# Weight check in three pieces, one logarithm scale per lane, rstd for four sequences at once, down copy on GpSimd, the branch turned round and a new order

## The chip, the cores and the metric

The kernel runs on one core of a Trainium2 chip. The metric is the device time of one execution in microseconds (us). A core has four compute engines with a queue each: TensorE (PE; its weight loads are PEld), VectorE (DVE), ScalarE (ACT) and GpSimd (POOL). SyncE (SP) issues most of the DMAs. Each queue runs in the order in which it is written, and waits on semaphores.

## The reference

```python
x = x + _wkv(time_decay, time_first, _layernorm(x), ctx_2048)      # (16, 128, 256)
x = x + _ffn(_layernorm(x), gate_w, up_w, down_w, gate_s, up_s, down_s)

# _wkv, for each sequence and channel, over the 128 steps:
w = -exp(time_decay); u = time_first; aa = bb = 0; pp = -1e38
q = maximum(pp, u + k_t)
y_t = (exp(pp - q) * aa + exp(u + k_t - q) * v_t) / (exp(pp - q) * bb + exp(u + k_t - q))
q2 = maximum(pp + w, k_t)
aa = exp(pp + w - q2) * aa + exp(k_t - q2) * v_t
bb = exp(pp + w - q2) * bb + exp(k_t - q2);  pp = q2

# _ffn: 256 -> 704 -> 256
hdn = silu((x @ gate_w.T) * gate_s) * ((x @ up_w.T) * up_s)
out = (hdn @ down_w.T) * down_s
```

The three weight matrices are drawn from -1, 0 and 1.

## The kernel before

The 16 sequences are cut into eight units of two sequences (256 tokens), and into four groups of two units (512 tokens) for the feed-forward part. A call such as `expk(3)` is one step of unit 3, `gate(7)` one step of tile 7. The hidden size 704 makes six tiles a group (five of 128, one of 64 for gate and up together), so tiles are numbered 0 to 23, six to a group.

For each unit: DVE takes the statistics of the layer norm (`stats1`, `aggr1`, lines 459 to 469); ACT makes the reciprocal standard deviation by a logarithm and an exponential (`rstd1`, L327, L329); POOL makes the bias (`bias1`, L234, L236); ACT takes exp of the normalised input (`expk`, L336) and POOL multiplies it by the values in units 0 to 3 (`weigh`, L242). PE transposes both (`e_T`, L600, and `p_T`, L609). DVE runs the recurrence as two scans (`scan_e`, L487, and `scan_p`, L498) and makes denominator and numerator (`denom`, L512, and `numer`, L522). ACT makes the reciprocal of the denominator as exp of minus the logarithm (`log_den`, L347, and `recip`, L354; one instruction for each half of the channels, since scale and bias differ between the halves). POOL multiplies and adds (`divide`, L258, and `add_y`, L264), which ends the first residual. Then PE transposes it (`x1_T`, L619), DVE takes the second statistics (`stats2`, `aggr2`), POOL or ACT the reciprocal standard deviation (`rstd2`, `rstd2a`), ACT normalises (`norm2`, L370), PE transposes back (`n_T`, L627), and ACT and DVE split the result into a high and a low part for the matmuls (`high_n`, L381, and `low_n`, L545).

The feed-forward part of a tile is `gate` and `up` (four matmuls of 512 columns each, L645), `silu` (ACT, L406), `gated` (DVE, L559), `high_h` (ACT, L417), `low_h` (POOL, L294), and `down` (four matmuls, L660); `finish` (DVE, L574) adds the second residual and SP stores it. `gate(0)` needs `low_n(0)` and `low_n(1)` and the rounded copy of the gate and up weights; `down(0)` needs that of the down weights.

The matmuls may use a faster number format only when the low 16 bits of every weight are zero, which is tested at run time. `wcheck` (ACT, L392) sums the low halves of the gate and up weights, then of the down weights; `wany_` (DVE, L453), `count` (PE, L668 and L669) and `publish` (DVE, L457) make one number of it. PE reads it into a register and branches (L695, L696). Its program from there on stands twice: the first body is for weights that are not exact, the second for exact ones. These weights are exact, so the second body runs:

```python
found = pe.value_load(flag[0:1, 0:1], min_val=0, max_val=2 * P)
with pe.If(found > 0):
    rest_of_program(False)
with pe.Else():
    rest_of_program(True)
pe.nop()
```

Before the branch PE does `e_T` and `p_T` of units 0 and 1 and `count`. The copies of the weights in the faster format are made by `whi`: the gate and up weights in four pieces on POOL (L286), the down weights in one on ACT (L397). The order of all steps on each engine is written out by hand (lines 297 to 303, 421 to 432, 577 to 588 and 681 to 689). ACT loads its function tables (L308) whenever it passes between exp or logarithm and silu.

Of the kernel before, what the change touches and what calls it, by code (L numbers as in the profile page):

```python
# [17 lines left out]
UB = 2  # L18
# [17 lines left out]
F_MAX = 55.0  # L36

# [13 lines left out]
def build(nc, x_tok, x_ch, v_tok, v_ch, w_gu, w_d, vecs, out_ch):  # L51
    with ExitStack() as ctx:
# [170 lines left out]
        def _(pool):  # L223
# [73 lines left out]
            bias1(0); weigh(0); bias1(1); weigh(1); whi(0); whi(1); whi(2); whi(3); first(0); divide(0); bias1(2)  # L297
            add_y(0); bias1(3); divide(1); add_y(1); weigh(2); bias1(4); weigh(3); rstd2(0); first(1); first(2)
            rstd2(1); divide(2); add_y(2); rstd2(2); divide(3); add_y(3); low_h(0); bias1(5); low_h(1); bias1(6)
            rstd2(3); low_h(2); divide(4); add_y(4); low_h(3); rstd2(4); divide(5); low_h(4); add_y(5); low_h(6)  # L300
            bias1(7); rstd2(5); low_h(7); first(3); divide(6); add_y(6); low_h(8); low_h(9); rstd2(6); low_h(10)
            divide(7); add_y(7); low_h(12); low_h(13); low_h(14); rstd2(7); low_h(15); low_h(16); low_h(18); low_h(19)
            low_h(20); low_h(21); low_h(22)

        @block.scalar
        def _(act):
# [24 lines left out]
            def expk(u):

                act.wait_ge(s_xt[u], 16)
                act.wait_ge(s_nb1, u + 1)
# [4 lines left out]
            def log_den(u):  # L339
                act.wait_ge(s_den, u + 1)  # L340
                if u == 0:
                    act.wait_ge(s_f, 2)
                if u >= 2:
                    act.wait_ge(s_y, u - 1)
                for c in range(CC):
                    q = slice(c * UB, (c + 1) * UB)
                    last = nc.scalar.activation(rden[:, u % 2, q, 1:T], den[:, u % 2, q, 1:T], ACT.Ln, scale=elift[:, c:c + 1])  # L347
                last.then_inc(s_ln, 1)

            def recip(u):  # L350
                act.wait_ge(s_ln, u + 1)
                for c in range(CC):
                    d = rden[:, u % 2, c * UB:(c + 1) * UB, 1:T]
                    last = nc.scalar.activation(d, d, ACT.Exp, scale=-1.0, bias=lift[:, c:c + 1])  # L354
                last.then_inc(s_rd, 1)
# [28 lines left out]
            def wcheck(k):  # L384

                act.wait_ge((s_wgu, s_wd)[k], 16)
                raw = wgu[:, :, :, :].rearrange("p c m n -> p (c m n)") if k == 0 else wd[:, :, :].rearrange("p m n -> p (m n)")
                n = (WGU_N, WD_N)[k]
# [354 lines left out]
```

## Time and profile before

| | us |
|---|---|
| median of 3 runs | 114.91 |
| lowest, highest | 114.43, 115.06 |
| the profiled execution, its own time | 114.74 |
| its span in the trace | 112.9 |
| PE, DVE, ACT, POOL busy | 83.7, 80.9, 83.7, 66.5 |
| TensorE's mean granted clock, of full speed | 0.977 |

The span runs from the first to the last record of the trace; the 1.8 us that are left lie around it. Busy times are of one execution; the time of a matmul is modelled, and matmuls overlap, so that the distance between two starts tells more than the duration of one. A letter q behind an engine (PEldq, SPq) marks its sequencer. "Issue" in a chain is time in which an engine waited for nothing that the profile shows.

### The profile page before, as it was taken

How to read it: one execution, taken by the hardware profiler on the slowest of the kernel's cores; microseconds unless marked ns; L12 is line 12 of the kernel's file. 1: busy time of each engine (PE TensorE's matmuls, PEld its weight loads, DVE VectorE, ACT ScalarE, POOL GpSimd, SP SyncE). 2: the span in 40 equal slices, each digit the busy share in tenths (PEclk: the TensorE clock that was granted, in tenths of full speed). 3: DMA queues.
4: the chain of work that ended last, by engine and by line, in shares of the span. 5: the costliest groups of instructions: out<-in, count | busy, mean ns of one | idle time of the engine just before them, and what ended most of it. 6: DMA issues, size and time to landing. Idle time of an engine off the chain costs nothing.

```text
span 112.9 us, 1463 instructions
## 1 busy us (share of the span) xinstructions
PE 83.7 (74%) x380; PEld 64.9 (57%) x380; DVE 80.9 (72%) x169; ACT 83.7 (74%) x157; POOL 66.5 (59%) x100
## 2 busy tenths in 40 slices
PE   0034700039249999997999989999999999999940
PEld 0022400039139778766688858876877777888810
DVE  1918989409997999997899999999385266515270
ACT  4453999941998989899999989999984763555500
POOL 2025956890683259889559485795898720473600
PEclk9999999999976999999999999999999999999996
DMA  2999999991000000000000005000040000500005
GB/s 71 275 378 397 386 355 377 370 367 62 4 3 0 0 0 9 0 0 0 0 0 0 0 0 186 6 3 0 0 175 14 0 0 0 192 0 0 0 0 186
DMA packets 6458, 10.77 MB, mean 95 GB/s; under 512 B 560, under 2 KB 3632, under 8 KB 6320
## 3 DMA queue, kind: packets, MB, share of 16 engines
q1 hardware_dynamic: 6304, 10.62, 26.3%
q8 instruction: 5, 0.08, 0.3%
q10 hardware_dynamic: 144, 0.03, 0.2%
q14 instruction: 5, 0.04, 0.1%
HBM read 8.55 MB, written 2.10 MB: 94 GB/s over the span
## 4 chain that ended last, share of the span: by engine, by line
PE 35%; ACT 23%; POOL 13%; issue 10%; DMA 8%; DVE 6%; SPq 1%; DVEq 1%; POOLq 0%; ACTq 0%
PE ps_f L645 20%; PE ps_d L660 9%; DMA wgu<-w_gu 8%; POOL hl L294 3%; POOL yk L258 3%; ACT L308 3%; ACT rden L354 3%; ACT ek L336 3%; ACT junk L392 3%; ACT rden L347 2%; POOL xc L264 2%; PE ps_x L627 2%; ACT sil L406 2%; DVE sbe L487 2%; PE ps_a L600 2%
## 5 line engine op out<-in xcount | busy, mean ns | idle before, releaser
L645 PE MATMUL ps_f<-xh,wgu_r 128*128 128x512 f32 x88 | 35.8, 407 | 0.0
L645 PE MATMUL ps_f<-xl,wgu_r 128*128 128x512 f32 x88 | 34.8, 395 | 0.0
L294 POOL TENSOR_TENSOR hl<-h,hh 128x512 fp32r<-128x512 f32 x20 | 25.7, 1293 | 10.5 <-ACT hh L417 10.3
L559 DVE SCALAR_TENSOR_TENSOR h<-ps_f,vec,sil 128x512 f32<-128x512 f32 (+1 forms) x24 | 17.9, 748 | 10.5 <-PE ps_f L645 5.8
L645 PEld LDWEIGHTS ps_f<-xh,wgu_r 128*128 128x128 f32 x88 | 16.5, 188 | 4.9 <-ACT sil L406 0.4
L600 PE MATMUL ps_a<-ident,ek 128*128 128x128 f32 x32 | 7.2, 368 | 15.9 <-ACT ek L336 8.0
L645 PEld LDWEIGHTS ps_f<-xl,wgu_r 128*128 128x128 f32 x88 | 16.6, 188 | 3.4
L660 PE MATMUL ps_d<-hh,wd_r 128*128 128x512 f32 x40 | 16.5, 412 | 0.4 <-POOL hl L294 0.3
L406 ACT ACTIVATE sil<-ps_f,vec 128x512 f32<-128x512 f32 x20 | 13.6, 688 | 3.0 <-PE ps_f L645 2.9
L660 PE MATMUL ps_d<-hl,wd_r 128*128 128x512 f32 x40 | 15.8, 394 | 0.0
L417 ACT ACTIVATE hh<-h 128x512 fp32r<-128x512 f32 x20 | 12.3, 627 | 4.3 <-DVE h L559 4.0
L487 DVE TENSOR_TENSOR_SCAN sbe<-decay,ps_a 128x512 f32<-128x512 f32 x8 | 9.7, 1215 | 7.8 <-PE ps_a L600 7.6
L600 PEld LDWEIGHTS ps_a<-ident,ek 128*128 128x128 f32 x32 | 5.1, 190 | 17.2 <-ACT ek L336 8.6
L258 POOL TENSOR_TENSOR yk<-num,rden 128x508 f32<-128x508 f32 x8 | 10.2, 1274 | 6.4 <-DVE num L522 3.3
L336 ACT ACTIVATE ek<-xt,nb,rs 128x256 f32<-128x256 f32 x16 | 8.7, 590 | 3.4 <-POOL nb L236 3.4
L308 ACT ACT_TABLE_LOAD x8 | 10.3, 1283 | 1.3 <-PEq L737 1.2
L264 POOL TENSOR_TENSOR xc<-xc,yk 128x508 f32<-128x508 f32 x8 | 10.2, 1279 | 0.6
L347 ACT ACTIVATE rden<-den,elift 128x254 f32<-128x254 f32 x16 | 7.2, 498 | 4.1 <-DVE den L512 4.0
L498 DVE TENSOR_TENSOR_SCAN sbp<-decay,ps_b 128x512 f32<-128x512 f32 x8 | 9.7, 1207 | 0.4 <-issue 0.2
L660 PEld LDWEIGHTS ps_d<-hh,wd_r 128*128 128x128 f32 x40 | 7.5, 188 | 3.0 <-POOL hl L294 1.4
L660 PEld LDWEIGHTS ps_d<-hl,wd_r 128*128 128x128 f32 x40 | 7.5, 188 | 1.5
L370 ACT ACTIVATE nt<-ps_x,nb,rs 128x256 f32<-128x256 f32 x14 | 7.1, 558 | 1.6 <-POOL nb L280 1.6
(72 smaller groups left out, 132.5 us busy)
## 6 DMA issues: line engine op xcount, KB each, us to landing
xt<-x_tok SPq DMA_DIRECT2D x8, 256.0 KB, 10.5
xc<-x_ch SPq DMA_DIRECT2D x4, 512.0 KB, 11.4
out_ch<-xc SPq DMA_DIRECT2D x8, 256.0 KB, 2.5
wgu<-w_gu SPq DMA_DIRECT2D x1, 1408.0 KB, 9.3
vt<-v_tok SPq DMA_DIRECT2D x2, 512.0 KB, 9.2
vc<-v_ch SPq DMA_DIRECT2D x2, 512.0 KB, 9.8
wd<-w_d SPq DMA_DIRECT2D x1, 768.0 KB, 10.6
vec<-vecs ACTq DMA_DIRECT2D x1, 25.0 KB, 2.3
```

Of the source, the lines that this page charges most:

```text
L258: nc.gpsimd.tensor_tensor(yk[:, u % 2, :, 1:T], num[:, u % 2, :, 1:T], rden[:, u % 2, :, 1:T], ALU.mult).then_inc(s_y, 1)
L264: nc.gpsimd.tensor_tensor(later(xc, u), later(xc, u), yk[:, u % 2, :, 1:T].rearrange("p (c b) t -> p c b t", c=CC), ALU.add).then_inc(s_x1, 1)
L294: nc.gpsimd.tensor_tensor(hl[:, m, :], h[:, n % HS, :], hh[:, m, :].bitcast(F32), ALU.subtract).then_inc(s_hl, 1)
L308: nc.scalar.preload_act_table_set(name)
L336: last = nc.scalar.activation(ek[:, b, :], xt[:, b, :], ACT.Exp, scale=rs1[:, b:b + 1], bias=nb1[:, b:b + 1])
L406: nc.scalar.activation(sil[:, n % 2, :], f, ACT.Silu, scale=vec[:, V_GS + m:V_GS + m + 1]).then_inc(s_sil, 1)
L417: nc.scalar.activation(hh[:, m, :], h[:, n % HS, :], ACT.Copy).then_inc(s_hh, 1)
L487: nc.vector.tensor_tensor_scan(sbe[:, u % 2, :, :].rearrange("p q t -> p (q t)"), decay[:, :, :].rearrange("p q t -> p (q t)"), ps_a[:, :, ...
L559: nc.vector.scalar_tensor_tensor(h[r, n % HS, :], ps_f[r, slot(n, 1) % RING, :], vec[r, V_US + m:V_US + m + 1], sil[r, n % 2, :], ALU.mult ...
L600: last = nc.tensor.transpose(ps_a[:, c * UB + b, :], ek[:, u * UB + b, c * P:(c + 1) * P], ident[:, :])
L645: last = nc.tensor.matmul(ps_f[:, i % RING, :], w, a, start=c == 0 and x is xh, stop=c == CC - 1 and x is xl)
L660: last = nc.tensor.matmul(ps_d[:, c, :], wd_r[:, m, cs] if exact else wd[:, m, cs], a if exact else a.bitcast(F32), start=m == 0 and i == ...
```

## The change

1. `wcheck` is done in three pieces: the two halves of the gate and up weights, then the down weights; `wany` and `count` have three columns.
2. `lift` is one number per lane, from the larger `tfc` of the two halves, so that `log_den` and `recip` are one instruction each for all four rows; this takes one more DVE instruction at the start.
3. `rstd1` and `bias1` are done for units 0 and 1 singly, then for units 2 and 3, 4 and 5, 6 and 7 together (`pair`).
4. `whi` of the down weights moves from ACT to POOL, in two pieces of 768 columns, which are whi(4) and whi(5).
5. The branch asks `found < 1`, and the exact body comes first.
6. The order of the steps is new on POOL, ACT, DVE and PE.

```diff
+        def pair(u):
+            return (seqs(u), u + 1) if u < GU else (slice((u - 1) * UB, (u + 1) * UB), u // GU + GU)
...
             def bias1(u):
+                q, k = pair(u)
+                pool.wait_ge(s_rs1, k)
+                nc.gpsimd.tensor_tensor(mr1[:, q], mv1[:, q, 0], rs1[:, q], ALU.mult).then_inc(s_mr1, 1)
...
             def rstd1(u):
                 act.wait_ge(s_mv1, u + 1)
...
+                q, k = pair(u)
+                nc.scalar.activation(lv1[:, q], mv1[:, q, 1], ACT.Ln, bias=epsc[:, 0:1]).then_inc(s_lv1, 1)
...
-                act.wait_ge(s_nb1, u + 1)
+                act.wait_ge(s_nb1, u + 1 if u < GU else u // GU + GU)
...
-                for c in range(CC):
-                    q = slice(c * UB, (c + 1) * UB)
-                    last = nc.scalar.activation(rden[:, u % 2, q, 1:T], den[:, u % 2, q, 1:T], ACT.Ln, scale=elift[:, c:c + 1])
-                last.then_inc(s_ln, 1)
+                nc.scalar.activation(rden[:, u % 2, :, 1:T], den[:, u % 2, :, 1:T], ACT.Ln, scale=elift[:, 0:1]).then_inc(s_ln, 1)
...
-                act.wait_ge((s_wgu, s_wd)[k], 16)
-                raw = wgu[:, :, :, :].rearrange("p c m n -> p (c m n)") if k == 0 else wd[:, :, :].rearrange("p m n -> p (m n)")
+                act.wait_ge(s_wgu if k < CC else s_wd, 16)
+                raw = wgu[:, k, :, :].rearrange("p m n -> p (m n)") if k < CC else wd[:, :, :].rearrange("p m n -> p (m n)")
...
-            def whi(_):
-                act.wait_ge(s_wd, 16)
-                nc.scalar.activation(wd_r[:, :, :], wd[:, :, :], ACT.Copy).then_inc(s_wdr, 1)
...
+                    pool.wait_ge(s_wd, 16)
+                    q = slice((i - 4) * (MC // 2), (i - 3) * (MC // 2))
+                    nc.gpsimd.tensor_copy(wd_r[:, q, :], wd[:, q, :]).then_inc(s_wdr, 1)
...
-            with pe.If(found > 0):
+            with pe.If(found < 1):
+                rest_of_program(True)
+            with pe.Else():
                 rest_of_program(False)
-            with pe.Else():
-                rest_of_program(True)
             pe.nop()
```

The new order on POOL, ACT, DVE and PE, up to where the feed-forward part starts (the lists go on in the same manner):

```diff
+            bias1(0); weigh(0); bias1(1); weigh(1); whi(0); whi(4); whi(1); whi(2); first(0); whi(5); bias1(3)
+            divide(0); add_y(0); divide(1); add_y(1); first(1); whi(3); weigh(2); rstd2(0); bias1(5); rstd2(1)
+            weigh(3); divide(2); add_y(2); rstd2(2); divide(3); add_y(3); low_h(0); low_h(1); low_h(2); first(2)
...
+            rstd1(0); expk(0); rstd1(1); expk(1); wcheck(0); wcheck(1); wcheck(2); log_den(0); rstd1(3); recip(0)
+            log_den(1); expk(2); recip(1); expk(3); rstd1(5); rstd2a(0); log_den(2); recip(2); rstd2a(1); norm2(0)
+            norm2(1); expk(4); high_n(0); high_n(1); log_den(3); expk(5); recip(3); tables(SILU); silu(0); silu(1)
...
+            stats1(0); aggr1(0); stats1(1); aggr1(1); scan_e(0); denom(0); scan_p(0); numer(0); scan_e(1); stats1(2)
+            stats1(3); aggr1(2); aggr1(3); wany_(); denom(1); publish(); scan_p(1); stats1(4); numer(1); stats1(5)
+            aggr1(4); scan_e(2); aggr1(5); stats2(0); aggr2(0); denom(2); stats2(1); aggr2(1); scan_e(3); scan_p(2)
+            numer(2); denom(3); stats1(6); low_n(0); low_n(1); stats1(7); stats2(2); scan_p(3); aggr2(2); numer(3)
...
+                e_T(2); x1_T(0); x1_T(1); e_T(3); p_T(2); n_T(0); n_T(1); e_T(4); p_T(3); x1_T(2); gate(0); gate(1)
+                up(0); up(1); up(2); gate(2); n_T(2); gate(3); up(3); gate(4); x1_T(3); down(0); gate(5); down(1)
```

Before, the same stretches read:

```python
# POOL, lines 297 to 299
bias1(0); weigh(0); bias1(1); weigh(1); whi(0); whi(1); whi(2); whi(3); first(0); divide(0); bias1(2)
add_y(0); bias1(3); divide(1); add_y(1); weigh(2); bias1(4); weigh(3); rstd2(0); first(1); first(2)
rstd2(1); divide(2); add_y(2); rstd2(2); divide(3); add_y(3); low_h(0); bias1(5); low_h(1); bias1(6)
# ACT, lines 421 to 423
rstd1(0); expk(0); rstd1(1); expk(1); wcheck(0); wcheck(1); log_den(0); recip(0); log_den(1); rstd1(2)
rstd1(3); expk(2); recip(1); expk(3); whi(4); log_den(2); rstd1(4); recip(2); rstd2a(0); expk(4)
rstd2a(1); norm2(0); norm2(1); rstd1(5); high_n(0); high_n(1); log_den(3); rstd1(6); recip(3)
# PE, lines 681 and 682
e_T(2); x1_T(0); x1_T(1); p_T(2); e_T(3); n_T(0); n_T(1); p_T(3); e_T(4); x1_T(2); gate(0); gate(1)
```

## Rows read from the trace of the kernel before

**Rows 1.** The page, busy time of each engine: us, share of the span, instructions.

```profile
PE 83.7 (74%) x380; PEld 64.9 (57%) x380; DVE 80.9 (72%) x169; ACT 83.7 (74%) x157; POOL 66.5 (59%) x100
```

**Rows 2.** Windows of five stretches: busy us (instructions) per engine, granted clock, DMA share, GB/s.

```profile
16.90:24.30 7.40, 0.00 (x0) 0.00 (x0) 3.96 (x16) 6.56 (x15) 5.92 (x9) 1.00 1.07 376
24.30:36.50 12.20, 8.45 (x40) 7.62 (x41) 10.02 (x26) 8.28 (x25) 6.32 (x12) 0.86 0.13 47
36.50:80.00 43.50, 42.04 (x198) 32.03 (x197) 40.83 (x77) 41.90 (x75) 31.09 (x46) 1.00 0.04 13
80.00:108.50 28.50, 28.35 (x127) 22.25 (x125) 13.83 (x22) 16.64 (x26) 16.08 (x16) 1.00 0.10 38
```

**Rows 3.** Lines 695 and 696, TensorE's sequencer: ns min/median/max, then first and last start in us.

```profile
L695 PEldq TENSOR_LOAD <-flag x1: 489/489/489, 17.0 to 17.0; - x1
...
L696 PEldq COMPARE_BRANCH  x1: 6323/6323/6323, 17.9 to 17.9; - x1
```

**Rows 4.** DMA queues, 16.9 to 24.3 us: packets, MB, share of 16 engines.

```profile
q1 hardware_dynamic: 1797, 2.77, 105.8%
q8 instruction: 1, 0.02, 0.9%
```

**Rows 5.** Timeline from 11 to 37 us: start, duration, engine, line, operation, [idle before].

```profile
11.52 2.55 ACT L392 ACTIVATE junk<-wgu 128x2816 bf16<-128x2816 uint16 x1 [0.34 <-DMA wgu<-w_gu]
...
14.25 1.48 ACT L392 ACTIVATE junk<-wd 128x1536 bf16<-128x1536 uint16 x1
...
16.72 0.14 DVE L457 CAST flag<-ps_d 1x1 int32<-1x1 f32 x1
...
19.50 1.09 ACT L336 ACTIVATE ek<-xt,nb,rs 128x256 f32<-128x256 f32 x2 [0.21 <-POOL nb L236]
...
22.86 1.27 POOL L264 TENSOR_TENSOR xc<-xc,yk 128x508 f32<-128x508 f32 x1
24.08 1.27 POOL L242 TENSOR_TENSOR vt<-vt,ek 128x512 f32<-128x512 f32 x1
...
24.34 1.09 PE L600 MATMUL ps_a<-ident,ek 128*128 128x128 f32 x4 [7.93 <-issue]
...
25.54 1.22 DVE L487 TENSOR_TENSOR_SCAN sbe<-decay,ps_a 128x512 f32<-128x512 f32 x1 [4.61 <-PE ps_a L600]
...
31.34 0.87 DVE L522 SCALAR_TENSOR_TENSOR num<-ps_b,fcol,sbp 128x254 f32<-128x254 f32 x2
...
32.68 1.12 PE L627 MATMUL ps_x<-ident,nt 128*128 128x128 f32 x4 [3.71 <-ACT nt L370]
...
36.52 0.48 PE L645 MATMUL ps_f<-xh,wgu_r 128*128 128x512 f32 x1
```

**Rows 6.** The chain of waits, late part: start us, us, what.

```profile
80.09 0.44 PE ps_x L627 x4
...
94.76 4.67 PE ps_f L645 x20
```

**Rows 7.** Groups by line, whole kernel: count | busy us, mean ns | idle before, releaser.

```profile
L417 ACT ACTIVATE hh<-h 128x512 fp32r<-128x512 f32 x20 | 12.3, 627 | 4.3 <-DVE h L559 4.0
...
L347 ACT ACTIVATE rden<-den,elift 128x254 f32<-128x254 f32 x16 | 7.2, 498 | 4.1 <-DVE den L512 4.0
...
L286 POOL CAST wgu_r<-wgu 128x704 fp32r<-128x704 f32 x4 | 2.9, 774 | 0.0
...
L327 ACT ACTIVATE lv<-mv,epsc 128x2 f32<-128x2 f32 x8 | 2.3, 290 | 1.3 <-DVE mv L468 1.3
...
L397 ACT ACTIVATE wd_r<-wd 128x1536 fp32r<-128x1536 f32 x1 | 1.5, 1467 | 0.0
```

**Rows 8.** Line 52, the end of the block: ns min/median/max, then first and last start.

```profile
L52 PEldq DRAIN  x1: 785/785/785, 108.0 to 108.0; - x1
...
L52 SPq COMPARE_BRANCH  x1: 33/33/33, 112.6 to 112.6; - x1
```

More of the change, by code:

```diff
@@ L344, in log_den @@
                     act.wait_ge(s_y, u - 1)
-                for c in range(CC):
-                    q = slice(c * UB, (c + 1) * UB)
-                    last = nc.scalar.activation(rden[:, u % 2, q, 1:T], den[:, u % 2, q, 1:T], ACT.Ln, scale=elift[:, c:c + 1])
-                last.then_inc(s_ln, 1)
+                nc.scalar.activation(rden[:, u % 2, :, 1:T], den[:, u % 2, :, 1:T], ACT.Ln, scale=elift[:, 0:1]).then_inc(s_ln, 1)
             def recip(u):
                 act.wait_ge(s_ln, u + 1)
[L352 to L355, printed above, removed]
+                d = rden[:, u % 2, :, 1:T]
+                nc.scalar.activation(d, d, ACT.Exp, scale=-1.0, bias=lift[:, 0:1]).then_inc(s_rd, 1)
             def rstd2a(u):
@@ L425, in _ @@
-            tables(LN_EXP); log_den(4); expk(5); expk(6); high_h(2); recip(4); norm2(3); high_h(3); log_den(5)
-            high_n(3); recip(5); tables(SILU); silu(4); silu(5); high_h(4); silu(6); norm2(4); high_h(5); silu(7)
-            high_h(6); high_n(4); high_h(7); silu(8); silu(9); tables(LN_EXP); rstd1(7); log_den(6); expk(7); norm2(5)
-            recip(6); high_n(5); tables(SILU); silu(10); silu(11); high_h(8); high_h(9); silu(12); high_h(10)
-            high_h(11); silu(13); tables(LN_EXP); log_den(7); norm2(6); recip(7); high_h(12); high_h(13); high_n(6)
@@ new lines, in _ @@
+            norm2(1); expk(4); high_n(0); high_n(1); log_den(3); expk(5); recip(3); tables(SILU); silu(0); silu(1)
+            norm2(2); high_h(0); silu(2); high_n(2); high_h(1); silu(3); high_h(2); silu(4); tables(LN_EXP)
+            log_den(4); rstd1(7); recip(4); norm2(3); expk(6); high_n(3); high_h(3); log_den(5); recip(5)
+            tables(SILU); silu(5); silu(6); high_h(4); high_h(5); norm2(4); silu(7); high_h(6); high_n(4); silu(8)
+            high_h(7); silu(9); tables(LN_EXP); expk(7); log_den(6); high_h(8); norm2(5); recip(6); high_n(5)
@@ L575, in finish @@
                                                    xc[:, c, ts], ALU.mult, ALU.add).then_inc(s_fin, 1)
-            stats1(0); aggr1(0); stats1(1); aggr1(1); scan_e(0); denom(0); scan_p(0); numer(0); scan_e(1); scan_p(1)
-            wany_(); denom(1); publish(); stats1(2); aggr1(2); stats1(3); aggr1(3); numer(1); stats1(4); stats1(5)
-            aggr1(4); scan_e(2); denom(2); stats2(0); stats1(6); aggr2(0); stats2(1); aggr1(5); aggr2(1); scan_p(2)
-            numer(2); scan_e(3); aggr1(6); denom(3); low_n(0); low_n(1); scan_e(4); stats2(2); aggr2(2); scan_p(3)
@@ L588, in _ @@
+            gated(10); gated(11); mulp(7); stats2(6); aggr2(6); denom(7); scan_p(7); gated(12); numer(7); gated(13)
+            low_rest(11); gated(14); low_n(6); finish(1); stats2(7); aggr2(7); gated(15); gated(16); gated(17)
+            low_n(7); low_rest(17); gated(18); finish(2); gated(19); gated(20); gated(21); gated(22); gated(23)
             low_rest(23); finish(3)
@@ L651, in down_ @@
                 if n == 0:
[L652 removed]
+                    pe.wait_ge(s_wdr, 2)
                 if m == 0 and g >= 1:
@@ L667, in count @@
                 pe.wait_ge(s_wany, 1)
-                nc.tensor.matmul(ps_d[0:1, 1, 0:1], ones[:, :], wany[:, 0:1], start=True, stop=False)
-                nc.tensor.matmul(ps_d[0:1, 1, 0:1], ones[:, :], wany[:, 1:2], start=False, stop=True).then_inc(s_wcnt, 1)
+                for k in range(CC + 1):
+                    last = nc.tensor.matmul(ps_d[0:1, 1, 0:1], ones[:, :], wany[:, k:k + 1], start=k == 0, stop=k == CC)
+                last.then_inc(s_wcnt, 1)
             def rest_of_program(exact):
```

92 lines of the change are left out of this document (41 added, 51 removed).

## The prediction, made before the changed kernel was run

> **What bounds the kernel now.** I read the page's busy times first. PE and ACT are both busy for 74% of the span and DVE for 72% [rows 1], so no engine bounds the whole; the stretches have to be read apart. The windows do that [rows 2]. From 80 to 108.5 us PE is busy for 28.35 of 28.5 us, and the chain there is PE's alone: twenty matmuls take 4.67 us, which is 0.2335 us each, and a group of four transposes takes 0.44 us [rows 6]. From 36.5 to 80 us PE is busy for 42.0, ACT for 41.9 and DVE for 40.8 of 43.5 us: three engines are nearly full at once. From 24.3 to 36.5 us PE waits much, and from 16.9 to 24.3 us it has no instruction at all, while the DMA queues are full.
>
> How full is PE from its first product on? `gate(0)` starts at 36.52 [rows 5], and the sequencer drains from 108.0 to 108.8 us [rows 8]. Between them lie 66 product steps and downs of four matmuls (44 gates and ups; 20 full downs and four half ones make 22): 264 x 0.2335 = 61.6 us; and 14 groups of transposes (three `e_T`, five `x1_T`, six `n_T`): 6.2 us. Of 36.5 to 108.5, 72.0 us, this leaves 4.2 us for gaps and switches. So what comes before `gate(0)` passes to the end nearly one for one, and everything after it has at most 4.2 us to give.
>
> The empty 7.4 us is the main reading. PE's sequencer loads the flag at 17.0, starts its compare-and-branch at 17.9 and spends 6.3 us in it, until 24.2 [rows 3]; `e_T(2)` starts at 24.34, and DVE has been idle for 4.61 us before its scan at 25.54 [rows 5]. Its operand is ready much earlier: `expk(2)` ends at 19.50 + 1.09 = 20.59. In this time one packet of instructions came in, 0.9% of 16 x 7.4 us, so 1.1 us long, among data at 105.8% of the queues' time [rows 4]. The exact body is the second one, so the branch is a jump over the first body, and its instructions had to be fetched.
>
> **The branch turned round.** With the exact body first, the sequencer falls through. No row shows a branch on PE that isn't a jump out of what is loaded. Bounds: 6.3 us, the row of PE, and about nothing, SP's compare-and-branch at 0.033 us [rows 8]. I take the low one, because the difference is the fetch. A jump then stands at the other end: after the last `down` PE must pass the whole body that isn't used. Its sequencer is done at 108.0 and SP, which waits for the last store, at 112.6 [rows 8], so 4.6 us are covered. Bounds for what sticks out: nothing, or 6.3 - 4.6 = 1.7, with the drain of 0.8 behind it 2.5 us. The 6.3 us were measured in full data queues, while at the end only the last two stores are under way; I take nothing. The Trainium skill, "Runtime: NRT & Kernel Launch", section "Instruction fetch mechanics", has this rule: prefetch is purely sequential, and a taken branch to a target outside the window stalls until a DMA has brought its page. By that rule the change removes one stall and adds another, at the end; it gives the second rival a chance of its own.
>
> **The check and the flag.** Pieces: 2816 columns take 2.55 us and 1536 take 1.48 [rows 5], so 0.84 ns a column, and 1408 columns take 1.37. Two of them are 0.2 us more than one large one, and one more readout of some 0.2 us goes with it: the check ends 0.4 us later. DVE now does the statistics of units 2 and 3 ahead of `wany_`, in the place where `scan_p(1)` was; by my walk they end as the check ends (16.2). If xt(3) lands late they cost up to 0.9 us, which `expk(2)` covers. Third count matmul, one more `lift` instruction: tenths at most, covered by the check and by the wait for the first input. The cast of the flag moves from 16.72 to 17.1 [rows 5], the branch from 17.9 to 18.3 [rows 3].
>
> **ACT before e_T(2).** Two instructions of 254 columns are 2 x 0.498 us [rows 7] as records, 0.9 in time since they overlap. One of 508 columns isn't in the trace: at most those 0.9, at least about the 0.627 of a 512-column copy [rows 7]. I take 0.63, so 0.28 saved a pair. Ahead of `expk(2)` lie three such pairs (0.8 saved) and one `rstd1` less (a logarithm of 0.29 [rows 7] and an exponential of about 0.2), against the 0.4 of the check: 20.59 + 0.4 - 0.8 - 0.5 = 19.7 us. The bias must be there too: POOL has `whi(5)` just ahead of `bias1(3)`, a piece of 768 columns at 0.774 x 768/704 = 0.84 us [rows 7], and gets to it at about 17.4, in time. So `e_T(2)` starts at **19.7 instead of 24.34**, 4.6 us earlier, set by ACT and no longer by the branch (18.3).
>
> **From e_T(2) to gate(0).** POOL is late next. `divide` and `add_y` of units 0 and 1 are 4 x 1.27 us from 17.9: x1(1) is there at 23.0, against 24.1 before. Then come `first(1)` and `whi(3)` (0.77), and `weigh(2)` ends at 25.1, no earlier than before (24.08 + 1.27) [rows 5]. From there: `p_T(2)` 1.1, `scan_p(2)` 1.2 and `numer(2)` 0.87: 28.3 us, where the row has 31.34 + 0.87 = 32.2. `divide(2)`, `add_y(2)`: 30.9. `x1_T(2)`: 31.8. Beside it ACT does `norm2`, `expk(4)` and `high_n`, and DVE ends `low_n(1)` at about 31.0. So `gate(0)` starts at **31.9 instead of 36.52: 4.6 us**. The 1.47 us of the down copy leave ACT [rows 7] where it then waited anyway; on POOL they are 1.7 us, most of it while POOL waited for xc(0) and for `recip(0)`. I cost both at nothing; without that cover `add_y(1)` and all behind it move by 0.8.
>
> **After gate(0).** All queues are as far ahead as PE: `expk(5)` and `stats1(7)` are done, which weren't. In the full stretch ACT loses eight pairs (8 x 0.28 = 2.2 us) and `expk(5)` (1.09 [rows 5]), which now lies ahead of it. That is taken from an engine which with DVE shares the bound, so it can give back only of PE's 4.2 us; part of these are switches and the last chain. Bounds: nothing and 3.3. DVE loses nothing there, hence I take a low value, 0.7.
>
> **Sum**, against the profiled execution (114.74, of which 112.9 are span; it is 0.17 below the median of 114.91): 114.74 - 4.6 - 0.7 = **109.4 us**.
>
> **Rivals.**
> 1. *The forecast*: chance 0.60, 107.2 to 110.6.
> 2. *The jump at the end sticks out.* The body that is skipped is about as far a jump as the one of 6.3 us. For it: same engine, same kind of jump. Against it: the queues are quiet and 4.6 us are covered. Up to 2.5 us: 111.9. Chance 0.12.
> 3. *Slow chain and slow clock before gate(0).* Before, PE idled for 3.71 us, then four transposes took 1.12 us at 32.68 [rows 5], where the late ones take 0.44 in the chain [rows 6]; the granted clock of that stretch is 0.86 [rows 2], so part of it ran at 1.2 GHz. In the new order PE works in short pieces up to 31.9 and may do its first products at the lower clock, at 1.87 us a step instead of 0.93: up to 1.7 us. If also the 4.3 us from the end of `numer(2)` to `gate(0)` stay as they are, that is 0.7 more (28.3 + 4.3 = 32.6). 109.4 + 2.4 = 111.8. Against it: DVE and ACT have less in the way. Chance 0.20.
> 4. *Slower: the branch costs its 6.3 us either way*, because the sequencer refills after any compare-and-branch, or because the program is laid out so that the first body too is reached by a jump. Then `e_T(2)` starts at 18.3 + 6.3 = 24.6 us, 0.3 later than before, the jump at the end adds up to 2.5, and the lighter ACT gives back 0.7: 114.74 + 0.3 + 2.5 - 0.7 = 116.8. It decides from the point where the branch's record is longer than some 5.5 us. For it: only that the trace has no short branch of PE. Against it: the packet of instructions. Chance 0.05.
> 5. *No difference*: the branch is short, and DVE or ACT holds the stretch to its old end. Chance 0.03.
>
> **The numbers.** The range of 107.2 to 112.3 holds the first three cases but for their tails; its low end takes 2.2 us more of PE's gaps, its high end rivals 2 and 3 with a little beyond. Faster by over 0.5% (about what a measurement of this kernel can tell from no change) 0.92, within it 0.03, slower 0.05.
>
> **What would show it.** The compare-and-branch under 0.3 us and `e_T(2)` near 19.7, right behind `expk(2)`; no packet of instructions between 17 and 24 us; the check ending near 16.2; `gate(0)` near 31.9; 0.6 to 0.65 us for the instructions of 508 columns; PE's drain near 103 and SP's last wait still on the store. I am wrong if the branch is still long, if `gate(0)` comes after 33, or if PE's sequencer is the last at the end.

## The result

| | before | changed |
|---|---|---|
| median, us | 114.98 | 110.34 |
| lowest, highest | 114.43, 115.22 | 110.25, 110.51 |
| the profiled execution, its own time | 114.74 | 110.51 |
| its span | 112.9 | 108.7 |

Four executions of each on the same chip. The ratio is 0.9605 (95% interval 0.9567 to 0.9642): 4.6 us less. The forecast was 109.4, 0.9 us lower, with a range of 107.2 to 112.3. In two of the runs below, e2 and e6, one execution lies over 1.5% above the fastest of its run: it counts in the median but not in the ratio, and without it the medians are 115.47 and 109.86.

The page's busy times of the changed kernel (they answer to [rows 1]: PE and DVE a little more, ACT 5.1 us less):

```profile
PE 85.4 (79%) x382; PEld 65.8 (61%) x382; DVE 83.3 (77%) x170; ACT 78.6 (72%) x136; POOL 67.7 (62%) x96
```

The branch first. This is the record of its line in the changed kernel, with times in ns (min/median/max) and the first and the last start in us; the same line number covers the compare-and-branch and the jump at the end of the body.

```profile
L702 PEldq COMPARE_BRANCH  x2: 86/1907/3728, 18.3 to 103.6; - x2
```

The compare-and-branch takes 86 ns at 18.3 us, where [rows 3] had 6323 ns at 17.9. The jump behind the last `down`, at 103.6 us, takes 3728 ns. No packet of instructions came in on TensorE's queue (q8) between 16.9 and 24.3 us, where [rows 4] had one. The timeline of the changed kernel shows what came of the short branch (start, duration, engine, line; the lines are those of the changed kernel, L349 `expk`, L605 `e_T`, L271 `add_y`, L249 `weigh`, L527 `numer`):

```profile
17.17 0.14 DVE L462 CAST flag<-ps_d 1x1 int32<-1x1 f32 x1
...
17.91 1.08 ACT L349 ACTIVATE ek<-xt,nb,rs 128x256 f32<-128x256 f32 x2
...
19.04 1.11 PE L605 MATMUL ps_a<-ident,ek 128*128 128x128 f32 x4 [2.13 <-ACT ek L349]
...
20.59 1.18 DVE L492 TENSOR_TENSOR_SCAN sbe<-decay,ps_a 128x512 f32<-128x512 f32 x1
21.27 1.25 POOL L271 TENSOR_TENSOR xc<-xc,yk 128x508 f32<-128x508 f32 x1
...
23.36 1.27 POOL L249 TENSOR_TENSOR vt<-vt,ek 128x512 f32<-128x512 f32 x1
...
27.36 0.87 DVE L527 SCALAR_TENSOR_TENSOR num<-ps_b,fcol,sbp 128x254 f32<-128x254 f32 x2
```

The flag is out at 17.17 + 0.14, `expk(2)` ends at 18.99, and `e_T(2)` starts at 19.04 right behind it, for 24.34 in [rows 5]. DVE's scan starts at 20.59 for 25.54. POOL ends `add_y(1)` at 22.5 (24.1 before), `weigh(2)` at 24.6 (25.35), and `numer(2)` ends at 28.2 (32.2). In windows at the new times (they answer to [rows 2]; the first is the same and the third as long, the second ends at the new `gate(0)` and is shorter):

```profile
16.90:24.30 7.40, 3.67 (x16) 2.74 (x16) 7.22 (x22) 5.17 (x12) 6.96 (x8) 1.00 1.07 377
24.30:31.70 7.40, 6.07 (x27) 4.55 (x26) 6.93 (x15) 7.32 (x17) 5.18 (x10) 1.00 0.15 56
31.70:75.20 43.50, 42.24 (x196) 33.16 (x195) 40.31 (x76) 38.33 (x61) 30.48 (x43) 1.00 0.04 13
75.20:104.30 29.10, 28.63 (x127) 22.27 (x125) 16.16 (x25) 16.80 (x27) 16.93 (x16) 1.00 0.10 37
```

PE has 3.67 us of work where it had none, and DVE 7.22 of 7.4 us where it had 3.96. In the 43.5 us from the first product on ACT is busy for 38.3, and was for 41.9. PE's queue at the start of the products looks so:

```profile
31.75 0.78 PE L650 MATMUL ps_f<-xh,wgu_r 128*128 128x512 f32 x1
32.32 0.63 PE L650 MATMUL ps_f<-xl,wgu_r 128*128 128x512 f32 x1
...
34.03 0.51 PE L650 MATMUL ps_f<-xl,wgu_r 128*128 128x512 f32 x1
34.38 0.39 PE L650 MATMUL ps_f<-xh,wgu_r 128*128 128x512 f32 x1
34.61 0.39 PE L650 MATMUL ps_f<-xl,wgu_r 128*128 128x512 f32 x1
34.84 0.40 PE L650 MATMUL ps_f<-xh,wgu_r 128*128 128x512 f32 x1
```

In the kernel before, the ninth of the same matmuls started at 38.48, where `gate(0)` started at 36.52:

```profile
38.48 0.40 PE L645 MATMUL ps_f<-xh,wgu_r 128*128 128x512 f32 x1
```

`gate(0)` starts at 31.75 for 36.52, 4.77 us earlier. But its matmuls follow each other at 0.43 us until 34.03, and at 0.23 us from 34.38 on: the first six ran at the lower of TensorE's two clocks, 1.2 GHz, the rest at 2.4. The nine first starts span 3.09 us, those of before 1.96. That is 1.13 us lost. The granted clock of the window says 1.00 all the same: this trace has no record of the clock before it rose, and the window counts that stretch as full speed, while the distance of the starts shows it.

And the end (ns, then first and last start), with the DMA queues from 103 us on:

```profile
L53 PEldq DRAIN  x1: 68/68/68, 107.4 to 107.4; - x1
L53 SPq COMPARE_BRANCH  x1: 33/33/33, 108.4 to 108.4; - x1
```

```profile
q1 hardware_dynamic: 288, 0.52, 25.1%
q8 instruction: 2, 0.03, 2.8%
```

PE's sequencer is done at 107.5 and SP at 108.4, after the last store. Two packets of instructions (q8) came in meanwhile; in the kernel before none came after 100 us.

### The profile page after: what moved, and what is told of

Read it like the earlier page. It is cut to its first block, busy times and chain, and to the rows that moved or that the text cites. A ratio compares the mean times of both kernels' runs of the same rounds, so it can differ in the third digit from the quotient of the medians.

```text
span 108.7 us, 1445 instructions
## 1 busy us (share of the span) xinstructions
PE 85.4 (79%) x382; PEld 65.8 (61%) x382; DVE 83.3 (77%) x170; ACT 78.6 (72%) x136; POOL 67.7 (62%) x96
## 4 chain that ended last, share of the span: by engine, by line
PE 59%; DVE 16%; ACT 9%; POOL 5%; issue 4%; DMA 2%; DVEq 1%; POOLq 0%; ACTq 0%
PE ps_f L650 36%; PE ps_d L665 13%; PE ps_a L605 3%; DVE sbe L492 3%; ACT L320 2%; POOL yk L265 2%; PE ps_x L624 2%; PE ps_x L632 2%; DMA vec<-vecs 2%; DVE sbp L503 2%; POOL xc L271 2%; DVE st L467 2%; DVE den L517 2%; DVE h L564 1%; DVE num L527 1%
## 5 line engine op out<-in xcount | busy, mean ns | idle before, releaser
L650 PE MATMUL ps_f<-xh,wgu_r 128*128 128x512 f32 x88 | 36.4, 413 | 0.1
L650 PE MATMUL ps_f<-xl,wgu_r 128*128 128x512 f32 x88 | 35.3, 401 | 0.0
L650 PEld LDWEIGHTS ps_f<-xh,wgu_r 128*128 128x128 f32 x88 | 17.1, 194 | 4.5 <-ACT sil L409 0.6
L650 PEld LDWEIGHTS ps_f<-xl,wgu_r 128*128 128x128 f32 x88 | 17.0, 193 | 3.7
L605 PE MATMUL ps_a<-ident,ek 128*128 128x128 f32 x32 | 7.3, 372 | 12.0 <-ACT ek L349 9.9
L420 ACT ACTIVATE hh<-h 128x512 fp32r<-128x512 f32 x20 | 12.2, 627 | 1.7 <-DVE h L564 1.6
L605 PEld LDWEIGHTS ps_a<-ident,ek 128*128 128x128 f32 x32 | 5.0, 188 | 13.9 <-ACT ek L349 12.5
L271 POOL TENSOR_TENSOR xc<-xc,yk 128x508 f32<-128x508 f32 x8 | 10.6, 1320 | 0.6
L349 ACT ACTIVATE ek<-xt,nb,rs 128x256 f32<-128x256 f32 x16 | 8.7, 594 | 2.1 <-POOL nb L243 2.1
L527 DVE SCALAR_TENSOR_TENSOR num<-ps_b,fcol,sbp 128x254 f32<-128x254 f32 x16 | 6.9, 473 | 0.2
```

The lines of the kernel that those rows point to most:

```text
L271: nc.gpsimd.tensor_tensor(later(xc, u), later(xc, u), yk[:, u % 2, :, 1:T].rearrange("p (c b) t -> p c b t", c=CC), ALU.add).then_inc(s_x1, 1)
L420: nc.scalar.activation(hh[:, m, :], h[:, n % HS, :], ACT.Copy).then_inc(s_hh, 1)
L605: last = nc.tensor.transpose(ps_a[:, c * UB + b, :], ek[:, u * UB + b, c * P:(c + 1) * P], ident[:, :])
L650: last = nc.tensor.matmul(ps_f[:, i % RING, :], w, a, start=c == 0 and x is xh, stop=c == CC - 1 and x is xl)
```

## The experiments

All times are medians. Each ratio is to the kernel before on the chip of the same run: e1 to e4 shared one chip, e5 to e8 another and e9 to e12 a third (medians of the kernel before 115.27, 115.07 and 115.20). The first table gives the times, and the second reads one profiled execution of each at three places: the start of `gate(0)`, what the first eight distances between matmul starts take over the 1.96 us that they take at full speed ("low clock"), and the time from `gate(0)` to the start of the last two matmuls less that loss ("net").

| run | median, us | ratio, 95% interval |
|---|---|---|
| changed | 110.34 | 0.9605 (0.9567 to 0.9642) |
| e1_branch_only | 111.49 | 0.9728 (0.9660 to 0.9797) |
| e2_branch_back | 115.69 | 1.0044 (0.9998 to 1.0090) |
| e3_two_logs | 110.42 | 0.9620 (0.9564 to 0.9675) |
| e4_no_branch | 110.53 | 0.9625 (0.9572 to 0.9679) |
| e5_warm | 109.14 | 0.9495 (0.9456 to 0.9533) |
| e6_down_act | 109.90 | 0.9533 (0.9488 to 0.9578) |
| e7_order_branch | 110.33 | 0.9595 (0.9554 to 0.9636) |
| e8_early_scan | 110.24 | 0.9607 (0.9560 to 0.9655) |
| e9_warm_down | 109.19 | 0.9458 (0.9426 to 0.9490) |
| e10_warm_copies | 109.87 | 0.9543 (0.9507 to 0.9578) |
| e11_branch_warm | 110.41 | 0.9591 (0.9550 to 0.9632) |
| e12_after_again | 110.52 | 0.9603 (0.9562 to 0.9644) |

| profiled execution | own time | `gate(0)` | low clock | net |
|---|---|---|---|---|
| before | 114.74 | 36.52 | 0.00 | 71.46 |
| changed | 110.51 | 31.75 | 1.13 | 70.76 |
| e1_branch_only | 110.92 | 32.54 | 0.00 | 71.49 |
| e2_branch_back | 115.45 | 36.91 | 1.01 | 70.75 |
| e3_two_logs | 109.72 | 31.88 | 0.33 | 70.79 |
| e4_no_branch | 109.67 | 31.98 | 0.18 | 70.76 |
| e5_warm | 108.24 | 30.77 | 0.00 | 70.72 |
| e6_down_act | 109.94 | 31.58 | 0.86 | 70.76 |
| e7_order_branch | 110.69 | 31.92 | 0.69 | 71.22 |
| e8_early_scan | 110.19 | 32.37 | 0.12 | 70.71 |
| e9_warm_down | 109.51 | 32.06 | 0.00 | 70.72 |
| e10_warm_copies | 109.61 | 31.09 | 0.00 | 71.65 |
| e11_branch_warm | 111.85 | 32.62 | 0.85 | 71.45 |
| e12_after_again | 110.56 | 31.76 | 1.30 | 70.75 |

**The branch alone.**

```diff
 # e1_branch_only, from the kernel before
-            with pe.If(found > 0):
-                rest_of_program(False)
-            with pe.Else():
-                rest_of_program(True)
+            with pe.If(found < 1):
+                rest_of_program(True)
+            with pe.Else():
+                rest_of_program(False)
```

> The kernel before with the branch turned round and nothing else. Theory (the 6.3 us of the branch are the gain): the compare-and-branch takes about 0.1 us, e_T(2) starts behind expk(2) at 20.7 instead of 24.34, the old order gives a little of it back (its PE queue has x1_T(1), which needs x1(1) at 24.1, ahead of p_T(2) and e_T(3)), gate(0) near 33.2, time about 111.6 us. Rival (the new order and the lighter ACT carry the gain, and the branch alone only exposes the next wait): at least 113.2 us.

Measured 111.49: 3.8 us of the 4.6 by the medians. The interval of its ratio lies above that of the changed kernel, so the rest of the change does add something once the branch is short: 1.1 us by the medians, 0.4 between the two profiled executions (this one is the fastest of its four). The branch's line:

```profile
L696 PEldq COMPARE_BRANCH  x2: 86/1837/3588, 17.8 to 104.0; - x2
```

86 ns again, and 3.6 us for the jump at the end. PE's timeline:

```profile
20.58 1.12 PE L600 MATMUL ps_a<-ident,ek 128*128 128x128 f32 x4 [4.23 <-ACT ek L336]
...
24.14 1.12 PE L619 MATMUL ps_d<-ident,xc 128*128 128x128 f32 x4 [1.58 <-POOL xc L264]
25.37 1.11 PE L609 MATMUL ps_b<-ident,vt 128*128 128x128 f32 x4
...
32.54 0.48 PE L645 MATMUL ps_f<-xh,wgu_r 128*128 128x512 f32 x1
```

`e_T(2)` is at 20.58 behind `expk(2)`, and `gate(0)` at 32.54: 4.0 us earlier than before, and with no product at the lower clock. The transposes behind `e_T(2)` wait for `add_y(1)` (24.14) and `weigh(2)` (25.37), as expected.

**The changed kernel with the old branch.** The edit is the reverse of the diff above, made in the changed kernel.

> The changed kernel with the branch as it was (exact body second). Theory: branch 6.3 us from 18.3, e_T(2) at 24.7, time about 114.3 us (112.5 is the least that rival allows). Rival (order and lighter ACT are worth half of the gain by themselves): about 112.5 us.

Measured 115.69, not faster than before, and 1.4 above what I expected. The branch and PE's timeline:

```profile
L702 PEldq COMPARE_BRANCH  x1: 6452/6452/6452, 17.9 to 17.9; - x1
```

```profile
24.51 1.09 PE L605 MATMUL ps_a<-ident,ek 128*128 128x128 f32 x4 [8.00 <-issue]
...
28.89 1.09 PE L605 MATMUL ps_a<-ident,ek 128*128 128x128 f32 x4 [1.59 <-DVE den L517]
29.77 1.06 PE L614 MATMUL ps_b<-ident,vt 128*128 128x128 f32 x4
...
36.91 0.78 PE L650 MATMUL ps_f<-xh,wgu_r 128*128 128x512 f32 x1
```

The branch costs 6.45 us, `e_T(2)` comes at 24.51 and `gate(0)` at 36.91, 0.4 later than before. The new order is made for an early start: it has `p_T(2)` behind `e_T(3)`, which waits until 28.89 for `denom(2)`, and so `p_T(2)` comes at 29.77, where the old order had it first (26.93). And the first products ran at the lower clock (1.01 us), which eats up the 0.71 us by which the net time is shorter. Without the short branch all the rest of the change gains nothing.

**Two logarithms.** Part 2 undone in the changed kernel:

```diff
 # e3_two_logs
-                nc.scalar.activation(rden[:, u % 2, :, 1:T], den[:, u % 2, :, 1:T], ACT.Ln, scale=elift[:, 0:1]).then_inc(s_ln, 1)
+                for c in range(CC):
+                    q = slice(c * UB, (c + 1) * UB)
+                    last = nc.scalar.activation(rden[:, u % 2, q, 1:T], den[:, u % 2, q, 1:T], ACT.Ln, scale=elift[:, c:c + 1])
+                last.then_inc(s_ln, 1)
 # and recip and lift likewise
```

> The changed kernel with two instructions again for log_den and for recip, one for each half of the channels (part 2 undone). ACT gets back 16 x about 0.28 = 4.5 us of work. Theory (ACT isn't the bound after gate(0)): e_T(2) about 0.8 later, of which DVE hides half; 110.7 us. Rival (ACT bounds the stretch of products): 112 us or more.

Measured 110.42: no difference. The net time is 70.79 us, as in the changed kernel. The shorter logarithms buy nothing by themselves that these runs show.

**No branch at all.** PE waits for the flag and always runs the exact body; the choice is left out.

```diff
 # e4_no_branch
-            found = pe.value_load(flag[0:1, 0:1], min_val=0, max_val=(CC + 1) * P)
-            with pe.If(found < 1):
-                rest_of_program(True)
-            with pe.Else():
-                rest_of_program(False)
+            rest_of_program(True)
```

> The changed kernel with neither the load of the flag nor the branch: PE still waits for the flag's semaphore and then always runs the exact body (left out: the choice between the bodies). Theory (what is left of the branch is covered at both ends, by expk(2) in front and by the last store behind): 110.3 us, within 0.2. Rival (the jump over the unused body at the end, 3.7 us long in the changed kernel, is in the way of the end): 109.5 us or less.

Measured 110.53, like the changed kernel, and its net time is the same. At the end PE's sequencer is idle early and SP is last all the same:

```profile
L53 PEldq DRAIN  x1: 785/785/785, 102.9 to 102.9; - x1
...
L53 SPq COMPARE_BRANCH  x1: 33/33/33, 107.5 to 107.5; - x1
```

From the start of the last two matmuls to the execution's full time it is 109.67 - 102.92 = 6.75 us here, and 110.51 - 103.64 = 6.87 in the changed kernel; before it was 114.74 - 107.98 = 6.76. The other runs show more than this pair. In the five executions whose last jump took 3.3 to 3.5 us (e3, e5, e6, e9, e12) this rest is 6.72 to 6.75, as without a jump; in the six where it took 3.6 to 3.8 us (changed, e1, e7, e8, e10, e11) it is 6.86 to 6.99. In the same six SP's issue of the last two stores took 1.16 to 1.41 us, and 0.99 to 1.05 in the other five. So 0.1 to 0.2 us go with a long jump. Whether the jump lengthens the issue or something else lengthens both is not shown.

**The clock at gate(0).**

```diff
 # e5_warm
+                def fill(k):
+                    for i in range(k):
+                        nc.tensor.transpose(ps_f[:, 2, 0:P], ident[:, :], ident[:, :])
-                e_T(2); x1_T(0); x1_T(1); e_T(3); p_T(2); n_T(0); n_T(1); e_T(4); p_T(3); x1_T(2); gate(0); gate(1)
+                e_T(2); x1_T(0); fill(6); x1_T(1); e_T(3); p_T(2); fill(3); n_T(0); n_T(1); fill(3); e_T(4); p_T(3); x1_T(2); gate(0); gate(1)
```

> The changed kernel with twelve transposes of the identity more, into a PSUM bank that nothing uses yet: six behind x1_T(0), three behind p_T(2), three behind n_T(1), where PE waited. Theory (in the changed kernel gate(0) starts at the lower of the two clocks, and six matmuls are 0.43 instead of 0.23 us apart, 1.2 us in all): with PE kept at work the granted clock is up before gate(0), and the time is 109.4 us. Rival (the rise doesn't depend on these gaps, or the fillers delay the transposes behind them by as much): 110.3 us or more.

Measured 109.14, 1.2 below the changed kernel, and its ratio's interval lies below that of the changed kernel. The profiled execution (108.24) is the fastest of its eight, so it shows more gain than the median. PE's timeline (L624 is `x1_T`, L680 the filler, L650 a product):

```profile
19.97 1.11 PE L624 MATMUL ps_x<-ident,xc 128*128 128x128 f32 x4
20.88 1.38 PE L680 MATMUL ps_f<-ident 128*128 128x128 f32 x6
22.54 0.66 PE L624 MATMUL ps_d<-ident,xc 128*128 128x128 f32 x4 [0.28 <-POOL xc L271]
...
30.36 0.66 PE L624 MATMUL ps_x<-ident,xc 128*128 128x128 f32 x4 [0.76 <-POOL xc L271]
30.77 0.48 PE L650 MATMUL ps_f<-xh,wgu_r 128*128 128x512 f32 x1
31.09 0.40 PE L650 MATMUL ps_f<-xl,wgu_r 128*128 128x512 f32 x1
```

Four transposes take 1.11 us at 19.97 and 0.66 at 22.54, so the clock is up by 22.5 us, where in the changed kernel it rose at about 34, and it stays up. `gate(0)` starts at 30.77, 1.0 earlier, and its second matmul follows at 0.32 us. Of the 1.0, 0.24 was there before any filler ran: `e_T(2)` starts at 18.80 for 19.04. From `e_T(2)` to `gate(0)` it is 11.97 us for 12.71. So the clock gives in two places in this execution: 0.7 us by shorter transposes on the way, and 1.13 by products that are not slow. The net time doesn't change (70.72). The medians keep 1.2 us of it.

**The down copy.** Part 4 undone in the changed kernel:

```diff
 # e6_down_act
-            ... whi(0); whi(4); whi(1); whi(2); first(0); whi(5); bias1(3)
+            ... whi(0); whi(1); whi(2); first(0); bias1(3)
-            ... recip(1); expk(3); rstd1(5); rstd2a(0); ...
+            ... recip(1); expk(3); whi_d(); rstd1(5); rstd2a(0); ...
 # and down(0) waits for one piece, not for two
```

> The changed kernel with the copy of the down weights on ACT again, behind expk(3), and the two pieces on POOL gone (part 4 undone). Theory (covered on either engine: ACT idled for 1.36 us behind expk(3), and POOL waited for xc(0)): 110.3 us, within 0.3. Rival (POOL's chain of divide and add_y gets the 1.6 us back): 109.6 us or less.

Measured 109.90, between the two forecasts; the intervals of its ratio and of the changed kernel's overlap. Its net time is that of the changed kernel. `gate(0)` is 0.17 earlier, but `e_T(2)` is 0.24 earlier already (18.80, as in e5, where the copy is on POOL). From there to `gate(0)` it is 12.78 us, 12.71 in the changed kernel and 12.78 in e12, which is the changed kernel again: the relief of POOL shortens nothing on this way. The run e9 below, which repeats it with the clock held up, gives 109.19 where the transposes alone gave 109.14. I take the copy as covered on either engine; the 0.4 us of the median are not explained.

**Order and branch alone.** Parts 1 to 4 undone together in the changed kernel: check in two pieces, two logarithms, single `rstd1` and `bias1` (each pair written as two steps), down copy on ACT.

> The new order and the branch turned round alone: check in two pieces, two logarithms, single rstd, down copy on ACT (parts 1 to 4 undone at once). Theory (these parts take work off engines that don't set the end): at most 0.5 us more than the changed kernel, 110.7 us. Rival (the parts make the order possible, and without them it is no better than the branch alone): 111.5 us or more.

Measured 110.33, the changed kernel's own time: by the medians parts 1 to 4 together are worth nothing, and the interval of the ratio lies below that of e1, so what the change adds to the short branch is in the order. In the profile the net time is 71.22, 0.46 above the changed kernel's; the lower clock cost 0.69 us there and 1.13 in the changed kernel, so that the two profiled executions end within 0.2 us of each other. The loss to the clock differs between executions (see below), so this is no reason for the equal medians.

**An earlier scan.**

```diff
 # e8_early_scan
-            aggr1(4); scan_e(2); aggr1(5); stats2(0); aggr2(0); denom(2); stats2(1); aggr2(1); scan_e(3); scan_p(2)
-            numer(2); denom(3); stats1(6)
+            aggr1(4); scan_e(2); denom(2); aggr1(5); stats2(0); aggr2(0); scan_e(3); stats2(1); aggr2(1); denom(3); scan_p(2)
+            numer(2); stats1(6)
-                e_T(2); x1_T(0); x1_T(1); e_T(3); p_T(2)
+                e_T(2); x1_T(0); e_T(3); x1_T(1); p_T(2)
```

> The changed kernel with denom(2) right behind scan_e(2), denom(3) ahead of scan_p(2), and e_T(3) ahead of x1_T(1) on PE, which waited 1.6 us for add_y(1) there. Theory (the chain to gate(0) goes through scan_e(3), scan_p(2) and e_T(4)): gate(0) 0.4 us earlier, 109.9 us. Rival (what is won goes into products at the lower clock, or POOL's weigh(3) and divide(2) hold x1_T(2) where it is): 110.3 us.

Measured 110.24, no gain, and the lower clock is not the reason (0.12 us): `gate(0)` comes at 32.37, 0.6 later.

```profile
22.64 1.08 PE L605 MATMUL ps_a<-ident,ek 128*128 128x128 f32 x4 [1.33 <-DVE den L517]
...
27.52 1.12 PE L632 MATMUL ps_x<-ident,nt 128*128 128x128 f32 x4 [1.54 <-ACT nt L378]
...
31.60 1.11 PE L624 MATMUL ps_x<-ident,xc 128*128 128x128 f32 x4 [0.23 <-POOL xc L271]
```

```profile
26.66 1.21 DVE L503 TENSOR_TENSOR_SCAN sbp<-decay,ps_b 128x512 f32<-128x512 f32 x1
...
28.93 1.27 POOL L265 TENSOR_TENSOR yk<-num,rden 128x508 f32<-128x508 f32 x1 [0.58 <-DVE num L527]
```

`e_T(3)` is at 22.64 instead of 23.73, but `stats2(1)` is now behind `scan_e(3)`, so `norm2` and `n_T(0)` are late (27.52 for 26.47). What sets `gate(0)` is another chain. On DVE `stats2(1)` and `denom(3)` both stand between `scan_e(3)` and `scan_p(2)` now, and `scan_p(2)` starts at 26.66 for 26.06. `numer(2)`, `divide(2)`, which waits for it, and `add_y(2)` each come 0.6 later with it, and `x1_T(2)`, the last step ahead of `gate(0)`, waits for `add_y(2)` and starts at 31.60 for 30.98. What `scan_e(3)` won, the steps moved in front of `scan_p(2)` took back and more.

**Both gains together, and POOL relieved.** e9 is e5 and e6 in one kernel. e10 also moves the last piece of the gate and up copy from POOL to ACT behind `expk(3)`, and the down copy behind `recip(3)`.

> The changed kernel with the twelve transposes that keep PE at work and the down copy back on ACT, both together. Theory (two different waits: the clock at gate(0), and POOL): the gains of the two runs add up, 108.9 us. Rival (the down copy made no difference, what was measured was spread between chips): 109.1 us, as with the transposes alone.

> As the run with the transposes and the down copy on ACT, but the last piece of the gate and up copy goes to ACT too, in its idle 1.4 us behind expk(3), so that POOL's weigh(2) and weigh(3) come 0.7 us earlier, and the down copy moves behind recip(3). Theory (POOL's chain add_y(1), weigh(2), weigh(3), divide(2), add_y(2) sets x1_T(2) and gate(0)): 108.6 us. Rival (scan_p(2) waits for scan_e(3) on DVE and not for POOL): no difference, 108.9 to 109.1 us.

e9: 109.19, the rival's number; nothing adds up. e10: 109.87, worse than both. Its `gate(0)` is 11.9 us behind its `e_T(2)` (31.09 and 19.18), in e9 it is 12.3 (32.06 and 19.78). But e5, without any relief of POOL, has 12.0 (30.77 and 18.80), so the 0.4 us are not POOL's. The clock rose later in e9: four transposes of `e_T(3)` take 1.06 us at 24.43 there, 0.63 at 23.65 in e10 and 0.63 at 23.48 in e5. What the relief did is seen in `weigh(2)`, which starts 3.8 us behind `e_T(2)` in e10 (22.98) and 4.5 in e5 (23.32), and what it did not do in `scan_p(2)`, here from e10 and then from e5:

```profile
25.77 1.20 DVE L513 TENSOR_TENSOR_SCAN sbp<-decay,ps_b 128x512 f32<-128x512 f32 x1
```

```profile
25.41 1.22 DVE L503 TENSOR_TENSOR_SCAN sbp<-decay,ps_b 128x512 f32<-128x512 f32 x1
```

Both are 6.6 us behind `e_T(2)`. `scan_p(2)` stands behind `scan_e(3)` on DVE and waits for that, as the rival of e10 said. And the net time of e10 is 0.9 longer. This is ACT's timeline (L410 the down copy, L320 a table load, L419 `silu`):

```profile
31.27 1.49 ACT L410 ACTIVATE wd_r<-wd 128x1536 fp32r<-128x1536 f32 x1
32.78 1.28 ACT L320 ACT_TABLE_LOAD   x1
34.08 1.27 ACT L419 ACTIVATE sil<-ps_f,vec 128x512 f32<-128x512 f32 x2
```

The copy stands ahead of the table load, and `silu(0)` starts at 34.08, 2.99 us behind `gate(0)`; in e9 it is at 33.56, 1.50 behind. The copy, which the idle 1.4 us behind `expk(3)` cover, delays `silu(0)` by its full length when it stands in front of it.

**The old order with fillers.** The same `fill` in e1, six behind `x1_T(0)` and six behind `e_T(3)`.

> The kernel before with the branch turned round, and six transposes of the identity behind x1_T(0) and six behind e_T(3), where its PE waited. Theory (with the old order PE's clock rose just before gate(0) at 32.5 us, so that no product was slow, but the transposes were): gate(0) 0.5 us earlier, 111.0 us. Rival (the clock, and not the new order, is what still parts this kernel from the changed one): 110.3 us or less.

Measured 110.41, as the rival said. The profiled execution (111.85) was one of two above 111 among six, whose others are 110.26 to 110.47. It shows what went wrong in it:

```profile
24.00:30.00 6.00, 3.19 (x23) 2.35 (x22) 5.89 (x20) 5.58 (x17) 5.49 (x12) 1.00 0.35 128
...
31.30:34.70 3.40, 3.40 (x13) 2.88 (x12) 3.37 (x8) 3.35 (x8) 0.35 (x2) 0.53 0.02 5
```

The clock rose early and fell again: PE was busy for 3.19 of the 6 us before 30, and the granted clock from 31.3 to 34.7 is 0.53, just where the first products are. `e12_after_again` is the changed kernel itself on the chip of e9 to e11:

> The changed kernel itself again, on the same chip as the three others, so that they can be compared within one call: 110.3 us, within 0.4.

110.52. So by the median the old order, with the short branch and fillers, comes to the changed kernel's time; e9, on the same chip, is better than that by 1.3 us in the medians (intervals of the ratios 0.9426 to 0.9490 and 0.9562 to 0.9644). How much of the order's 1.1 us over e1 is the order and how much the clock is therefore not settled.

## Why the prediction was right, and where it was off

- **The branch.** Right, and the two runs that exchange it alone settle it: with it turned round the old kernel gains 3.8 us, and without it the changed one gains nothing. It is 0.086 us and not 6.3; the low bound was the right one. That the difference is a fetch of instructions rests on the packets: one came between 16.9 and 24.3 us in both profiles of kernels that jump there, and none in the eleven of kernels that fall through.
- **The jump at the end.** Right: 3.7 us, of which 0.1 to 0.2 sticks out at most. The rule that I took from the Trainium skill ("Runtime: NRT & Kernel Launch", "Instruction fetch mechanics") agrees with the trace: the stall returns at the end, with two packets of instructions. It is shorter than at the front (6.3 and 6.5 us). There the queues were full of data; that this is the reason was not tested. The last store covers it because it is shorter: PE is done 0.9 us before SP, and 6.3 us from 103.6 on would have ended at 109.9, 1.5 us after SP. One of the signs I named failed, PE's drain near 103: the drain stands behind the jump and came at 107.4.
- **The flag.** Branch at 18.3, as said, but partly by luck. The check ended at 15.25 and not at 16.2, since the weights landed 8.3 us after their issue and not 9.3. That is spread between executions (8.1 to 9.5 in the runs here), not the change. The flag did not come earlier with it, because DVE does the statistics of units 2 and 3 ahead of `wany_`, which started at 15.83, 0.6 us behind the end of the check.
- **ACT before e_T(2).** 19.04 for 19.7: the check ended 0.95 earlier, and the three pairs saved 0.18 each and not 0.28. The check's pieces took 1.37 us each, as worked out. The instruction of 508 columns was mis-sized, 0.72 us for 0.63:

```profile
L358 ACT ACTIVATE rden<-den,elift 128x508 f32<-128x508 f32 x8 | 5.8, 719 | 0.8 <-DVE den L517 0.8
...
L400 ACT ACTIVATE junk<-wgu 128x1408 bf16<-128x1408 uint16 x2 | 2.7, 1370 | 0.1
```

- **To gate(0).** 31.75 for 31.9, but from `e_T(2)` on it took 12.7 us and not 12.2; the early start made up for the difference. `add_y(1)` ends at 22.5 for 23.0 and `weigh(2)` at 24.6 for 25.1, both 0.5 early: the walk through POOL is right so far, and `x1_T(1)` waited 1.56 us for it. But `numer(2)` ends at 28.2 for 28.3, hardly early. I had `scan_p(2)` behind `p_T(2)` alone; it stands behind `scan_e(3)` on DVE too, which started at 24.93 behind `e_T(3)` (23.73 to 24.82), and that was the later one:

```profile
24.69 1.12 PE L614 MATMUL ps_b<-ident,vt 128*128 128x128 f32 x4
...
24.93 1.22 DVE L492 TENSOR_TENSOR_SCAN sbe<-decay,ps_a 128x512 f32<-128x512 f32 x1
...
26.06 1.19 DVE L503 TENSOR_TENSOR_SCAN sbp<-decay,ps_b 128x512 f32<-128x512 f32 x1
```

- **After gate(0).** This term failed: I wrote -0.7, measured is +0.43 (71.46 to 71.89). The total stayed in the range all the same. It is two things. The net time fell by 0.70, just as taken. But the first products ran at the lower clock and lost 1.13. I had that as part of rival 3, at up to 1.7 us, and left it out of the sum. That 0.70 came out as taken is luck: I had chosen a low value between 0 and 3.3, for a reason that didn't hold (next point). Sum with what was measured: 114.74 - 4.77 - 0.70 + 1.13 + 0.11 at the end = 110.51.
- **The reason I gave for the 0.7** was ACT's relief. The two logarithms give none of it by themselves (e3), nor does the down copy (e6). Order and branch alone give 0.24 in one profiled execution (e7), all four parts together 0.46 more, of which the medians show nothing. Which of them is left open: parts 1 and 3 were not undone singly, and in e7 several small loads on ACT come together.
- Rival 2, rival 4 and rival 5 are out. Rival 3 was half true: slow clock, but not a slow chain from `numer(2)` to `gate(0)` (3.5 us, where it had 4.3).

## What to carry to other kernels

If a branch has a long record and a packet of instructions comes in during it, try the body that will run right behind it, and see to it that the jump over the other one falls where something else is awaited. After a stall has gone, look at TensorE's clock at the new first products: twelve transposes of the identity in its gaps cost little and gave 1.2 us here, and the distance of matmul starts shows the clock where the granted clock has no record. An order made for an early start can be worth nothing without that start (e2). And before a stretch of two profiles is compared, look at where it starts: in the kernels with the new order and the short branch `e_T(2)` came between 18.80 and 19.78, whatever was tried behind it.

## What the runs showed of the hardware

- A compare-and-branch on PE that falls through took 86 ns in all eleven profiles that have one. A jump over the other body took 6.3 and 6.5 us with the DMA queues full, with one packet of instructions, and 3.3 to 3.8 us with two stores under way, with two packets.
- The moment at which the clock rises isn't fixed. The changed kernel lost 1.13 and 1.30 us in two profiled executions, and two near twins of it, with nearly the same gaps on PE (e4, e3), 0.18 and 0.33. The Trainium skill says the same of the cost of a cold start in "TensorE: Matmul & The Clock Gate", Part 1: it varies from run to run. These executions agree, as far as single ones of each kernel can.
- A filler in the gaps can fail: in one execution (e11) the clock fell again, and its time, 111.85, is above the 111.49 of the same kernel without fillers.
- One ACT instruction of 508 columns takes 0.72 us, two of 254 columns 0.9; the readout of the sum another 0.19.
